# A post-norm attention and expert layer on one core: expert units loaded four ahead, a seventh half batch in expert order, side work between attention tiles in parts

## The chip, the cores and the metric

The program runs on 1 core of one Trainium2 chip. The metric is the device time of one execution in microseconds (us), and lower is better. The engines are TensorE (PE, with its weight loads shown as PEld), VectorE (DVE), ScalarE (ACT), GpSimd (POOL) and SyncE (SP), whose queue issues most DMAs.

## The reference

x has 4 batches of 1024 rows of 128 numbers, all in float32. One layer of attention and one of experts, each with a residual sum and a layer norm behind it:

```python
q, k, v = x @ Wq, x @ Wk, x @ Wv
latent = (k + v) @ W_down_kv
k_rec, v_rec = latent @ W_up_k, latent @ W_up_v
# 16 heads of 8 numbers
scores = clip(einsum(qh, kh) * scale) * exp(-0.0001 * |i - j|)
x = layernorm(x + (softmax(scores) @ vh) @ Wo)
top_logits, top_idx = top_k(x @ w_router, 2)          # 8 experts
h1 = x_e @ fc1_w[e]; proj, gate = split(h1)
out_e = (silu(proj) * gate) @ fc2_w[e]                # for the two experts of a row
moe = sum over the two of softmax(top_logits) * out_e
shared = (silu(x @ gate_w) * (x @ up_w)) @ down_w
x = layernorm(x + moe + shared)
```

## The kernel before, in words

The rows are cut into 8 **half batches** of 512 rows, c = 0 to 7. The kernel has two stages.

**Attention.** The work is 256 **tiles**, 32 in each half batch (32c + t, t = 0 to 31). A tile is one group of four heads (a quad, of which a half batch has four) and 128 keys against 512 queries. TensorE makes the scores into PSUM (L819), VectorE multiplies the diagonal band of a **crossing** tile (L1293; the tiles whose keys lie in the half batch of the queries), ScalarE makes two exponentials of 128x1024 (L714), and TensorE adds the probabilities times V into one output bank (L832). TensorE runs one tile ahead with its scores; three pairs of PSUM banks hold them. Keys and queries come in a split form with the decay multiplied in: GpSimd makes it (`split`, L535 to L537, twelve operations of a half batch), SP stores it into `stack_dram` (L386) and loads it back a quad at a time (`load_quad`, L379 and L381), two quads ahead of their use. SP issues in program order, and so the load of a quad stands behind the stores that the loop puts ahead of it (step g == 1 of each half batch).

**Side work.** Between tiles TensorE does one piece of other work for the half batch before (d = c - 1) and the one two ahead (p = c + 2), all in one PSUM bank, each piece after VectorE has taken the one before (`side`, `side_kept`). `beside` (from L897) places them by tile: `xT` (turn x, t = 1), the output turns `o` (t = 2, 10, 18, 26), `q` and `k` (projections of 512 columns, t = 3 and 5), `a` (turn, 4), `wo` (output projection, 6), `v` (7), `x` (turn the normed rows, 12), `lg` (router, 14), `norm` (15) and `cnt` (17). `cnt` counts the rows of each expert and waits for `chosen_ready`, which VectorE sets after it has found the two experts of each row (`route_lanes` and `choose`, taken at t = 16). GpSimd norms the rows (`ln1_rows`, L555 to L558) and makes a power (L568).

**Expert order.** For half batches 0 to 5 the rows are sorted by expert. The first GROUP is half batches 0 to 3 in 40 blocks of 128 rows, the second 4 and 5 in 24 blocks. When the counts are known VectorE works out each row's place (`order_counts` to `order_experts`), and GpSimd scatters rows into `sorted_dram` by indirect DMA (`send`, L574, 48 of 128 rows each). Half batches 6 and 7 are dense: every expert is applied to all rows and weighted.

**The ring stage.** After the last tile TensorE walks through a list `work` of pieces; each result takes the next of the eight PSUM banks in turn and is counted by `ring_ready`. The pieces: a **unit** is four blocks of the sorted rows (turn of its rows L774, up L980, down L994), a **shared** piece is the shared expert of one half batch (L985 with 8 matmul instructions, down L998 and L999), a **dense** piece one expert on 512 rows (L985 with 4, down L996). In the trace each float32 matmul stands as two. There are 16 units, 16 dense and 8 shared pieces. ScalarE copies and makes the silu (L738, L743, L748), VectorE multiplies (`hidden`, L1396) and adds dense and shared results (L1404, L1410). Five short steps of half batch 7 (`LAST_STEPS`) stand among the first pieces; `x` there waits for GpSimd's `ln1_rows(7)`.

A unit needs its rows (`load_rows`, L459, 256 KB) and its blocks' weights (`load_weights`, L466, four DMAs of 192 KB, each addressed by a register). There are two buffers of each, u % 2. SP's loop, in order, for unit u: load the rows of u + 2 (after the turn of u), load the weights of u + 2 (after the down of u), load 3 registers (L452), wait for ScalarE's copy of unit u's result, store it (L481). After ten units are stored GpSimd gathers the results of half batch 0 (`fetch`, L586, 8 indirect DMAs a half batch, each held back until the ring has come to an entry), then 1, 2, 3, and after all units 4 and 5; two half batches of gathered rows fit. VectorE weighs and adds them (`combine`, L1444) and makes statistics, GpSimd a power (L563, L564), ScalarE scales the rows (L724), SP stores them (L485).

## Time and profile before

| what | us |
|---|---|
| time, median of 3 runs | 804.7 |
| lowest and highest of the 3 | 801.01, 807.33 |
| the profiled execution, its own time | 802.82 |
| span of the profiled execution, first to last instruction | 800.9 |
| busy in it: PE, ACT, DVE, POOL | 675.2, 545.7, 333.2, 264.7 |

The time around the span is 802.82 - 800.9 = 1.9 us. In the trace the first exponential starts at 54.4 us and the last tile's matmuls end at 601.9 us, so the attention stage takes 547.5 us and the ring stage with the end 199.0 us. A row of the timeline gives start, duration, engine and line, the operation with its operands, how many instructions are merged, and in brackets how long the engine was idle before and which instruction or DMA released it. A row of the chain of waits has start, duration and what the chain went through there; its durations are exclusive, so that they can be summed. Line numbers are those of the kernel before.

### The profile page before, as it was taken

Reading aid. Unit: us, or ns where it says so; the run is one execution under the profiler, and the core shown is the slowest. Engines: PE = TensorE matmul, PEld = TensorE weight load, DVE = VectorE, ACT = ScalarE, POOL = GpSimd, SP = SyncE. Lnnn points to the kernel's source line nnn. Section 1 sums busy time; section 2 is a strip of 40 time slices with the busy share of each in tenths; the row PEclk is TensorE's granted clock in tenths of the full one; section 3 lists DMA queues with packets and bytes.
Section 4 is the critical chain, followed back from the end, with each engine's and each line's share of the span. In section 5 each row is a group of like instructions: output and inputs, shape, how many; then the busy total and the mean of one; then the engine's idle time right before and its main releaser. Section 6 shows DMA issues by size and latency. Waiting matters only on the chain.

```text
span 800.9 us, 12944 instructions
## 1 busy us (share of the span) xinstructions
PE 675.2 (84%) x4821; PEld 305.5 (38%) x4821; DVE 333.2 (42%) x989; ACT 545.7 (68%) x636; POOL 264.7 (33%) x250
## 2 busy tenths in 40 slices
PE   5029997999999999999999999999999878758980
PEld 3013322333333233333323333423337667646540
DVE  2913422443542244354525344433434412134883
ACT  2027996879789887978988899899993322223342
POOL 2800531720360171046227543044000100245672
PEclk9559998999999999999999999999999999888996
DMA  3799282274255227425423955243203665564131
GB/s 110 244 335 393 95 279 103 95 295 163 93 192 190 80 99 298 157 92 201 184 89 118 330 194 168 79 163 141 80 11 109 186 187 154 171 188 138 44 85 50
DMA packets 72883, 127.83 MB, mean 160 GB/s; under 512 B 6064, under 2 KB 48368, under 8 KB 72816
## 3 DMA queue, kind: packets, MB, share of 16 engines
q1 hardware_dynamic: 69216, 120.47, 43.4%
q0 software_dynamic: 3072, 6.30, 2.8%
q8 instruction: 40, 0.66, 0.3%
q10 hardware_dynamic: 528, 0.18, 0.1%
q14 instruction: 27, 0.22, 0.1%
HBM read 79.74 MB, written 48.76 MB: 160 GB/s over the span
## 4 chain that ended last, share of the span: by engine, by line
PE 59%; DVE 8%; issue 5%; ACT 4%; SPq 3%; DMA 3%; POOL 1%; another core or an unknown queue 0%; ACTq 0%; DVEq 0%
PE ps L832 22%; PE ps L819 16%; PE ps L985 5%; PE ps L774 4%; ACT probs L714 4%; PE ps L980 3%; DVE ps L1293 2%; DMA keys<-sorted_dram 2%; SPq L466 2%; PE ps L996 1%; PE ps L853 1%; PE ps L874 1%; DVE osb L1297 1%; PE ps L879 1%; PE ps L998 1%
## 5 line engine op out<-in xcount | busy, mean ns | idle before, releaser
L714 ACT ACTIVATE probs<-ps 128x1024 f32<-128x1024 f32 x512 | 479.3, 1053 | 103.8 <-DVE ps L1293 79.9
L832 PE MATMUL ps<-probs,V 128*9 128x512 f32 x2048 | 273.2, 606 | 1.2 <-ACT probs L714 0.4
L819 PE MATMUL ps<-queries,keys 32*128 32x512 f32 (+3 forms) x1408 | 199.5, 417 | 52.1 <-DMA queries<-stack_dram 39.2
L819 PEld LDWEIGHTS ps<-queries,keys 32*128 32x128 f32 x1408 | 98.4, 186 | 241.0 <-ACT probs L714 146.9
L1293 DVE TENSOR_TENSOR ps<-ps,cpk 128x256 f32<-128x256 f32 x256 | 103.2, 429 | 183.0 <-PE ps L819 177.1
L535 POOL TENSOR_TENSOR stage<-qk,rows_sb 128x512 fp32r<-128x512 f32 x28 | 36.8, 1314 | 183.9 <-DVE qk L1154 168.7
L586 POOL DMA_INDIRECT queries<-result_dram,slots x48 | 48.7, 1016 | 90.2 <-PE ps L980 68.1
L743 ACT ACTIVATE probs<-ps 128x512 f32<-128x512 f32 x48 | 28.5, 596 | 68.0 <-PE ps L985 33.4
L574 POOL DMA_INDIRECT sorted_dram<-xn,slots x48 | 47.0, 979 | 74.2 <-ACT probs L714 60.6
L1396 DVE TENSOR_TENSOR probs<-probs,ps 128x512 f32<-128x512 f32 x48 | 32.8, 687 | 86.0 <-PE ps L980 57.0
L985 PE MATMUL ps<-xnT,stage 128*128 128x512 f32 x128 | 59.0, 593 | 0.0
L1297 DVE COPY osb<-ps 128x512 f32<-128x512 f32 x32 | 22.1, 691 | 85.7 <-PE ps L832 85.7
L832 PEld LDWEIGHTS ps<-probs,V 128*9 128x9 f32 x2048 | 30.5, 88 | 58.5 <-issue 39.2
L980 PE MATMUL ps<-probs,keys 128*128 128x128 f32 x256 | 39.2, 319 | 0.0
L537 POOL TENSOR_TENSOR stage<-pool_f,stage 128x512 fp32r<-128x512 f32 x28 | 37.1, 1323 | 2.2
L980 PEld LDWEIGHTS ps<-probs,keys 128*128 128x128 f32 x256 | 37.6, 233 | 0.0
L536 POOL TENSOR_TENSOR pool_f<-qk,rows_sb 128x512 f32<-128x512 f32 x28 | 37.1, 1326 | 0.0
L555 POOL TENSOR_TENSOR small<-small 128x4 f32<-128x4 f32 x8 | 8.2, 1020 | 80.3 <-DVE small L1173 80.3
L545 POOL TENSOR_TENSOR squares<-qk 128x512 bf16<-128x512 f32 x16 | 17.0, 1082 | 51.1 <-DVE nmax L1269 50.9
L774 PE MATMUL ps<-cpk,keys 128*128 128x128 f32 x64 | 11.2, 303 | 26.7 <-DMA keys<-sorted_dram 26.7
L985 PEld LDWEIGHTS ps<-xnT,stage 128*128 128x128 f32 x128 | 22.5, 191 | 20.0 <-issue 18.6
L738 ACT ACTIVATE probs<-ps 128x512 f32<-128x512 f32 x16 | 9.5, 595 | 27.5 <-PE ps L774 27.5
(155 smaller groups left out, 540.4 us busy)
## 6 DMA issues: line engine op xcount, KB each, us to landing
stack_dram<-stage SPq DMA_DIRECT2D x64, 512.0 KB, 6.5
keys<-stack_dram SPq DMA_DIRECT2D x32, 1024.0 KB
queries<-stack_dram SPq DMA_DIRECT2D x32, 512.0 KB
keys<-expert_dram SPq DMA_DIRECT2D x64, 192.0 KB
sorted_dram<-y_pre SPq DMA_DIRECT2D x1, 4096.0 KB, 18.5
keys<-sorted_dram SPq DMA_DIRECT2D x16, 256.0 KB, 3.2
result_dram<-probs SPq DMA_DIRECT2D x16, 256.0 KB
x_tok<-in_L_attn_x SPq DMA_DIRECT2D x8, 256.0 KB, 5.8
```

What stands on the lines that cost most here:

```text
L535: rest(nc.gpsimd.tensor_tensor(hi, src, tab, ALU.mult))
L536: link(nc.gpsimd.tensor_tensor(pool_f[:, v, :], src, tab, ALU.mult))
L537: rest(nc.gpsimd.tensor_tensor(lo, pool_f[:, v, :], hi.bitcast(F32), ALU.subtract))
L574: pool.indirect_dma_start(out=sorted_dram, out_offset=bass.IndirectOffsetOnAxis(ap=slots[:, s, k:k + 1], axis=0), in_=xn[:, k // CT, tok(k ...
L586: pool.indirect_dma_start(out=gathered[:, c % 2, s, tok(t)], out_offset=None, in_=result_dram[0:rows, :], in_offset=bass.IndirectOffsetOnA ...
L714: nc.scalar.activation(probs[:, m % 3, 2 * j:2 * j + 2, :], ps[:, 2 * s:2 * s + 2, :], ACT.Exp, scale=SCALE).then_inc(exp_done, 1)
L774: last = nc.tensor.transpose(dst[:, tok(t)], src[:, tok(t)], ident)
L819: last = mm(bank[2 * s + i][:, lo:hi], keys[rows, u, kt // CT, v, tok(kt % CT)], queries[rows, u, v, lo:hi], start=True, stop=True)
L832: last = mm(bank[OUT_BANK][32 * i:32 * i + HD + 1, :], V[:, c // 2 % 2, kt, 4 * (Q % QUADS) + i, :], probs[:, m % 3, i, :], start=(kt == 0 ...
L980: last = mm(dst[:, tok(b)], wblk[:, u % 2, b, k * F:(k + 1) * F], xT_blk[:, u % 2, tok(b)], start=True, stop=True)
L985: last = mm(dst, up_sb[:, e, k * F:(k + 1) * F], xnT[:, c, :], start=True, stop=True)
L1293: tt(d, d, diag_fix.unsqueeze(1).to_broadcast([P, 2, P]), ALU.mult).then_inc(diag_done, 1)
```

## The change

- The second group is half batches 4, 5 and 6 in 32 blocks, 72 blocks in all. So there are 18 units, 8 dense and 8 shared pieces; half batch 6 has a `cnt` in attention (in half batch 7) and 8 more `send`s and gathers.
- Rows and weights of units have four buffers (`AHEAD`), in `pool_f`, `rows_sb`, parts of `keys` and `V`. The first two rows and the first weights are loaded before the last tile. 32 registers are loaded in half batch 7, and 4 a unit in the loop for ten units (3 before, for eleven).
- The pieces stand in another order, with all units ahead of all dense pieces, and so do the steps of half batch 7, the places of the combines and the gathers' hold-backs.
- The 24 sends of the second group stand in the ring stage, held back by `ring_ready`, and ahead of `ln1_rows(7)` on GpSimd. The 32 of the first group stand in half batches 5 and 6.
- Side work is placed by a table, `side_places`: `q`, `k`, `v`, `wo` and `lg` are done in two halves in neighbouring tiles, most jobs stand in tiles that don't cross, and `cnt` comes three tiles after `choose`. GpSimd splits the queries of p in one go before the keys; the splits of the keys stand behind `ln1_rows`.

```diff
-GROUPS = [(0, 4, 0, 40), (4, 6, 40, 64)]
+GROUPS = [(0, 4, 0, 40), (4, 7, 40, 72)]
...
+        AHEAD = 4
+        wblk = [w.rearrange("p (k n) -> p k n", k=UB) for w in (
+            rows_sb[:, :, :].rearrange("p v s -> p (v s)")[:, 0:UB * 3 * F], kflat[:, 0:UB * 3 * F], kflat[:, UB * 3 * F:2 * UB * 3 * F],
+            V[:, :, :, :, :].rearrange("p b t h d -> p (b t h d)")[:, 0:UB * 3 * F])]
...
+        def side_places(c):
...
+            z = 0 if c % 2 else 4
+            places = {("xT", p): (0 if c % 2 else 2,), ("o", 4 * d + 3): (z + (1 if c % 2 else 0),),
+                      ("q", p): (z + 2, z + 3) if c % 2 else (z + 1, z + 2), ("a", d): (6 if c % 2 else 7,),
+                      ("k", p): (z + 8, z + 9), ("wo", d): (z + 10, z + 11), ("o", 4 * c): (z + 13,),
+                      ("x", d): (z + 16,), ("norm", p): (z + 17,), ("lg", d): (z + 18, z + 19), ("o", 4 * c + 1): (z + 21,),
+                      ("cnt", d): (z + 24,), ("v", p): (z + 25, z + 26), ("o", 4 * c + 2): (z + 27,)}
...
-        for u in range(2 * GROUP - 2, UNITS, 2):
-            work += [("dense", GROUP, u // 2 - GROUP + 1), ("unit", u), ("unit", u + 1)]
...
+        shared_before = {0: 0, 4: 1, 8: 2, 12: 3, 15: 4}
+        work = []
+        for u in range(UNITS):
+            if u in shared_before:
+                work += [("shared", shared_before[u])]
+            work += [("unit", u)]
+        work += [("shared", c) for c in range(len(shared_before), GROUP)]
+        for c in range(GROUP, NCH):
+            work += [("dense", c, e) for e in range(E)] + [("shared", c)]
...
-        LAST_STEPS = {0: "o", 1: "a", 2: "wo", 4: "x", 5: "lg"}
+        LAST_STEPS = {0: "o", 1: "a", 2: "wo", 7: "x", 9: "lg"}
+        COMBINE_AFTER = {17: [0], 20: [1], 23: [2], 25: [3], 30: [4], len(work): [5, 6]}
...
-            n = ring["dn", "unit", GROUPS[0][3] // UB - 1][0] + (2 * CT * c + i) * 8 // 5
+            n = ring["dn", "unit", (FIRST_UNITS if c < GROUPS[0][1] else UNITS) - 1][0] + (2 * CT * (c % GROUPS[0][1]) + i) * 3 // 2
...
+            load_rows(0)
+            load_rows(1)
+            sp.wait_ge(experts_joined, 32)
+            load_weights(0)
+            sp.wait_ge(scores_ready, 2 * TILES)
+            load_weights(1)
+            load_rows(2)
+            load_weights(2)
+            load_rows(3)
+            sp.wait_ge(pv_done, TILES)
+            load_weights(3)
...
-                if u + 2 < UNITS:
-                    load_rows(u + 2)
-                    load_weights(u + 2)
-                if u < 11:
-                    load_registers(3)
+                if u + AHEAD < UNITS:
+                    load_rows(u + AHEAD)
+                    load_weights(u + AHEAD)
+                if u < 10:
+                    load_registers(4)
...
+            pool.wait_ge(slots_ready, 3)
+            for k in range(GROUPS[0][1] * CT, GROUP * CT):
+                send(k, ring_ready, 3 * (k - GROUPS[0][1] * CT))
             ln1_rows(LAST)
             gap_power(LAST)
...
+            def project(p, n, part):
+                dst = side(("qk"[n], p)) if part == 0 else bank[SIDE_BANK]
+                cols = slice(part * HALF // 2, (part + 1) * HALF // 2)
+                last = mm(dst[:, cols], wfold[:, 2, :] if n else Wq_sb[:, :], xT[:, p % 2, cols], start=True, stop=True)
```

On TensorE in half batch 1, from the router matmul (`Wr_sb`) to the count (`chosen`), the order before; a pair of L819 and L832 rows is a tile:

```order
160 L879 MATMUL ps<-Wr_sb,xnT 128x8 x4
161 L819 MATMUL ps<-queries,keys 128x512 x4
162 L832 MATMUL ps<-probs,V 9x512 x4
163 L865 MATMUL ps<-squares,head_sum_h 32x512 x2
164 L819 MATMUL ps<-queries,keys 128x512 x4
165 L832 MATMUL ps<-probs,V 9x512 x4
166 L819 MATMUL ps<-queries,keys 128x512 x4
167 L832 MATMUL ps<-probs,V 9x512 x4
168 L886 MATMUL ps<-chosen,cpk 128x40
```

The same place after, up to the count; L809 and L822 are now the tile's lines, and L764 is an output turn:

```order
184 L822 MATMUL ps<-probs,V 9x512 x4
185 L764 MATMUL ps<-cpk,osb 128x128 x4
186 L809 MATMUL ps<-queries,keys 128x384 x2
187 L809 MATMUL ps<-queries,keys 128x128 x2
188 L809 MATMUL ps<-queries,keys 128x384 x2
189 L809 MATMUL ps<-queries,keys 128x128 x2
190 L822 MATMUL ps<-probs,V 9x512 x4
191 L809 MATMUL ps<-queries,keys 128x512 x4
192 L822 MATMUL ps<-probs,V 9x512 x4
193 L809 MATMUL ps<-queries,keys 128x512 x4
194 L822 MATMUL ps<-probs,V 9x512 x4
195 L880 MATMUL ps<-chosen,cpk 128x40
```

The router matmul is now two halves (rows 174 and 177 of the same list), and five tiles lie between the second half and the count where three lay before.

On SP in the loop of the ring stage, the end of one unit's weights up to the next rows, before (`block_e` is what a register is loaded from):

```order
189 L466 ISA
190 L466 DMA keys<-expert_dram 128x384
191 L452 TENSOR_LOAD block_e
192 L452 ISA x2
193 L452 TENSOR_LOAD block_e
194 L452 ISA x2
195 L452 TENSOR_LOAD block_e
196 L452 ISA x2
197 L481 DMA result_dram<-probs 128x4x128
198 L459 DMA keys<-sorted_dram 128x4x128
```

The same place after:

```order
206 L423 ISA
207 L423 DMA rows_sb<-expert_dram 128x384
208 L409 TENSOR_LOAD block_e
209 L409 ISA x2
210 L409 TENSOR_LOAD block_e
211 L409 ISA x2
212 L409 TENSOR_LOAD block_e
213 L409 ISA x2
214 L409 TENSOR_LOAD block_e
215 L409 ISA x2
216 L479 DMA result_dram<-probs 128x4x128
217 L416 DMA pool_f<-sorted_dram 128x4x128
```

One register load more stands in each turn of the loop, and what is loaded is four units ahead.

On GpSimd from the last sends to the first gathers, before:

```order
126 L574 DMA sorted_dram<-xn,slots 8192x128 x16
127 L555 TENSOR_TENSOR small<-small 128x4
128 L557 TENSOR_TENSOR xn<-y_pre,small 128x512
129 L558 TENSOR_TENSOR xn<-xn,small 128x512
130 L568 TENSOR_TENSOR small<-small 128x4
131 L555 TENSOR_TENSOR small<-small 128x4
132 L557 TENSOR_TENSOR xn<-y_pre,small 128x512
133 L558 TENSOR_TENSOR xn<-xn,small 128x512
134 L568 TENSOR_TENSOR small<-small 128x4
135 L586 DMA queries<-result_dram,slots 128x128 x16
```

And after:

```order
129 L566 TENSOR_TENSOR small<-small 128x4
130 L573 DMA sorted_dram<-xn,slots 9216x128 x24
131 L553 TENSOR_TENSOR small<-small 128x4
132 L555 TENSOR_TENSOR xn<-y_pre,small 128x512
133 L556 TENSOR_TENSOR xn<-xn,small 128x512
134 L566 TENSOR_TENSOR small<-small 128x4
135 L585 DMA queries<-result_dram,slots 128x128 x16
```

The last sends, 24 of them, now stand directly ahead of the norm of half batch 7's rows.

## Rows read from the trace of the kernel before

**Rows 1.** Busy time by stretch; columns: length, PE, PEld, DVE, ACT, POOL, clock, DMA share, GB/s.

```profile
54.40:124.60 70.20, 61.79 (x450) 20.70 (x454) 22.65 (x51) 59.65 (x65) 19.11 (x16) 0.91 0.76 273
...
335.40:404.30 68.90, 64.55 (x504) 23.60 (x500) 32.27 (x101) 60.16 (x66) 29.15 (x26) 1.00 0.45 164
404.30:474.00 69.70, 65.60 (x504) 23.51 (x500) 28.85 (x87) 60.06 (x66) 36.84 (x35) 0.98 0.48 170
...
538.10:600.90 62.80, 61.15 (x476) 20.81 (x468) 23.73 (x79) 59.72 (x65) 12.00 (x13) 1.00 0.25 91
601.90:734.00 132.10, 105.43 (x665) 88.90 (x662) 40.54 (x107) 38.13 (x64) 25.18 (x26) 0.90 0.55 163
734.00:783.00 49.00, 43.90 (x201) 26.96 (x199) 41.46 (x151) 17.58 (x37) 34.66 (x38) 1.00 0.27 73
```

**Rows 2.** The chain of waits in two neighbouring tiles without side work.

```profile
520.45 0.98 PE ps L832 x8
522.28 0.98 PE ps L832 x8
```

**Rows 3.** Timeline of PE at the end of half batch 0.

```profile
123.67 0.80 PE L819 MATMUL ps<-queries,keys 32*128 32x512 f32 x4 [4.99 <-DMA queries<-stack_dram]
```

**Rows 4.** Timeline of SP there: the load of the quad behind the stores.

```profile
99.66 12.14 SPq L386 DMA_DIRECT2D stack_dram<-stage  x8
111.92 1.14 SPq L379 DMA_DIRECT2D keys<-stack_dram  x1
```

**Rows 5.** Timeline of PE at the count of half batch 5.

```profile
446.07 0.41 PE L886 MATMUL ps<-chosen,cpk 128*128 128x40 f32 x2 [1.47 <-issue]
...
448.99 1.12 PE L774 MATMUL ps<-cpk,osb 128*128 128x128 f32 x4
```

**Rows 6.** Waits of the ring stage: total us, times, longest.

```profile
PE ps L774 <- DMA keys<-sorted_dram: 26.7, 7, 6.6
```

**Rows 7.** The chain of waits in the ring stage: TensorE's pieces.

```profile
610.12 0.22 PE ps L999 x2
...
627.67 1.79 PE ps L980 x16
...
633.93 0.89 PE ps L994 x8
634.82 0.44 PE ps L774 x4
635.26 3.44 PE ps L985 x8
...
642.99 3.38 PE ps L980 x16
...
739.75 1.72 PE ps L985 x4
```

**Rows 8.** Timeline of SP: weights, result and rows in one turn of the loop.

```profile
635.01 1.93 SPq L466 DMA_DIRECT2D keys<-expert_dram  x4
638.66 0.39 SPq L481 DMA_DIRECT2D result_dram<-probs  x1
639.09 0.50 SPq L459 DMA_DIRECT2D keys<-sorted_dram  x1
```

**Rows 9.** The chain of waits: two register loads of SP.

```profile
653.58 0.26 SPq L452
654.13 0.26 SPq L452
```

**Rows 10.** Timeline of POOL: the first of the three operations that norm half batch 7.

```profile
619.36 1.01 POOL L555 TENSOR_TENSOR small<-small 128x4 f32<-128x4 f32 x1 [47.54 <-DVE small L1173]
```

**Rows 11.** The chain of waits at the end: last gathers, last combine.

```profile
779.89 1.00 POOL queries L586
...
781.19 3.85 DMA queries<-result_dram,slots
785.07 1.15 DVE qk L1444 x4
```

More of the change, by code:

```diff
@@ L618, in _ @@
                     split(0, p, 0)
+                    split(0, p, 1)
+                    split_end()
+                    pool.wait_ge(side_kept, numbers["k", p])
+                    squares_of(p)
                 if d >= 0:
@@ L1462, in _ @@
                     last_step(k)
-                if k and work[k - 1] == ("shared", GROUP):
-                    dve.wait_ge(ring_by_dve, ring["dn", "shared", GROUP][2])
-                    ln2_statistics(GROUP)
-                if k in COMBINE_AFTER:
-                    combine(COMBINE_AFTER[k])
-                    ln2_statistics(COMBINE_AFTER[k])
+                for c in COMBINE_AFTER.get(k, []):
+                    combine(c)
+                    ln2_statistics(c)
             dve.wait_ge(ring_by_dve, ring["dn", "shared", LAST][2])
```

384 lines of the change are left out of this document (169 added, 215 removed).

## The prediction

> **What bounds the kernel now.** I read the busy time by stretch first [rows 1]. The attention stage (54.4 to 601.9 us) is TensorE and ScalarE together: in half batch 7 (538.1 to 600.9) PE is busy 61.2 and ACT 59.7 of 62.8 us. The chain of waits has neighbouring plain tiles 522.28 - 520.45 = 1.83 us apart, with TensorE in it [rows 2]. 32 such tiles make 58.6 us. Half batch 7 takes 4.2 us more than that, half batch 5 (404.3 to 474.0) takes 69.7 - 58.6 = 11.1 more, half batch 4 10.3. That excess is side work and what it makes late. Two places in it are plain waits. At the end of half batch 0 TensorE stands 4.99 us for a quad [rows 3], whose load SP issued at 111.92, behind eight stores that took from 99.66 to 111.8 [rows 4]. And at the count of half batch 5 it stands 1.47 us; the output turn after it takes 1.12 us [rows 5].
>
> The ring stage (601.9 to 800.9) is 199.0 us. To 734 PE is busy 105.4 of 132.1 us at a granted clock of 0.90 [rows 1]. Its waits are seven for the rows of a unit, 26.7 us together, the longest 6.6 [rows 6]. The timeline of SP says why: the rows of the unit after next are issued only behind the weights, the register loads and the result of the unit before (639.09 behind 638.66 behind 635.01) [rows 8], and TensorE has by then done what it had. After such a wait the up of a unit takes 3.38 us where 1.79 is usual: the lower clock level, 1.2 GHz in place of 2.4 [rows 7]. From 734 to 783 VectorE is busy 41.5 of 49 us [rows 1], and the end is gathers, combine, statistics and scaling: the last gather lands at 785.07, 15.8 us before the end of the span [rows 11].
>
> **The change part by part: attention.**
> (a) The quad wait. The keys of half batch 2 are split later now (their projection stands at tiles 12 and 13), but the queries' stores go out before and only four stores stand ahead of the load. At about 2 us a tile the key split is over near 97 us, its four stores at 12.14 / 8 = 1.5 us each near 103, and the load is needed at about 118. The 4.99 us go, and about 0.9 us of slow tiles behind them: -5.9.
> (b) The count waits. By the order the count now stands five tiles behind the router's matmuls instead of three, and three behind `choose`. Odd half batches lose 1.47 us and the lower clock behind it. The clock of 0.98 over 69.7 us [rows 1] is 2.8 us at half speed, 1.4 us lost. 2.9 in each of half batches 1, 3 and 5, 8.6; in the even ones, where the excess is 0.8 smaller, I take 0.5 each for three (bounds 0 and 1). -10.
> (c) Side work in halves. No row shows a halved job. It may cost 0.2 us more for the second weight load and start at each of five jobs (1 us in each of six half batches, +6); it may save, since the smaller bites fit in the slack of three score buffers: the eight jobs of half batch 7 stand apart already, and of the eight, five turns at 4 x 0.15, two of 1 us and the router, about 5.6 us of matmuls cost 4.2, a quarter hidden. A quarter of 11 in six is -16. I take 0, between the ends: part of that quarter is in the measured excess already. Both ends stay for the range, +6 and -10.
> (d) One more count in half batch 7: +1.2. The later split in even half batches ends about 11 us before its quad is issued late; nothing waits by my sum.
> Sum -15 (bounds -6, if halves only cost and part of the clock loss stays, and -25): the last tile ends at 587.
>
> **The ring stage.** TensorE's pieces [rows 7]: unit 0.44 + 1.79 + 0.89 = 3.12; dense 1.72 + 0.89 = 2.61 (its down has as many instructions as a unit's); shared 3.44 + 8 x 0.22 = 5.2; the five last steps 3.1. Before: 16 x 3.12 + 16 x 2.61 + 8 x 5.2 + 3.1 = 136.4. After: 18 x 3.12 + 8 x 2.61 + 41.6 + 3.1 = 121.7. So 14.7 us of work go.
> The waits for rows go too: the rows of u + 4 are issued three units ahead of their turn. What is late next?
> - SP. A turn of its loop costs 4 x 0.52 (weights; 1.93 with the gap to the next) + 4 x 0.55 (two register loads are 654.13 - 653.58 apart [rows 9]) + 0.43 + 0.55 = 5.3 us; TensorE needs a unit each 3.12 + 5.2 / 4 = 4.4. Four units in hand at the start last for about 4 / (1 - 4.4 / 5.3) turns, over 20, and the register loads end after ten. It holds, with some small waits about units 8 to 13. But SP stores the results, and so unit 9 is stored late: first turn at 587 + 11.9 (turn, shared, two ups, down, steps) + 4.7 = 603.7, nine turns of 5.3 on: 651.5, landed near 654.5 (3 us, an estimate by the gather's 3.85 with its issue [rows 11]).
> - DMA. A unit moves 256 + 768 + 256 KB = 1.31 MB. The stretch to 734 moved 163 GB/s at a share of 0.55, so 296 at 1.0 [rows 1]. That is 4.4 us a unit, just TensorE's pace, with 0.22 us for each of 24 sends and 32 gathers beside. Over 18 units about 92 us against 88 for TensorE: a few us.
> - GpSimd's row norm. The last send waits for ring entry 35, and `x` of half batch 7 is entry 38, 0.9 + 0.9 us of matmuls later. Behind the send (1.3) come three operations of 1.1 [rows 10]: x is late by 1.3 + 3.3 - 1.8 = 2.8 to 3.7 us. It was hidden before.
> - The first combine. It stands in VectorE's queue behind piece 17, which TensorE reaches near 587 + 80 = 667. Eight gathers from 654.5 at 1.30 (781.19 - 779.89) are issued by 665, the last lands 2.9 later, combine and statistics are 4: VectorE is back at 672 at best, and all `hidden` products wait behind it. TensorE stands 5 us, up to 13 if gathers queue behind loads. I take 8.
> TensorE's end: 587 + 121.7 + 3.5 + 8 + 3.4 (slow clock after both) + 4 (SP, DMA) + 3 (VectorE, 85% busy in the dense pieces) = 730.6.
> - GpSimd's chain is longer. From 654.5: 56 x 1.30 = 72.8, six powers between at 1.5 = 9, so the last is issued at 736.3 and has landed at 739.2. Then the 15.8 us of the end [rows 11], since the fifth half batch is combined by then: 755.0.
> Span 755; with 1.9 us around it **757 us**, against 802.8 of the profiled execution, 46 less: 15 in attention and 31 in the ring stage. To the median of the runs shown, 804.7, the profiled one stands 2 lower; I leave that inside the range.
>
> **A rule against it.** In the stretch to 783 gathers stand at 1.00 us and 1.30 apart beside a VectorE that is 85% busy [rows 1, 11]. The Trainium skill, SBUF — State Buffer, section SBUF: two separate sides, says that a VectorE instruction in a two-port mode keeps GpSimd from writing the descriptors of its DMAs. By that rule the gathers would crawl beside combines; by the rows they don't, and the sum stays. What it would do here is the third rival.
>
> **The rivals.**
> 1. *Attention gains only its plain waits.* Halves cost their 6 us and the count's clock loss stays: 587 becomes 596 and the time 766. For it: TensorE is 95% busy there and a job's time is a job's time. Against: half batch 7 hides a quarter. 0.17.
> 2. *The unit stage becomes a queue.* SP's turns and the DMA engines, at 0.9 and more, stretch each other (a turn of 5.3 becomes 6.3, as the weights' issue is slower when the queue is full: the stores at 1.5 us each show that [rows 4]). Unit 9 is stored 9 us later, the combine wait doubles, and GpSimd's chain begins at 664: 757 + 9 to 757 + 20, say 771. For it: demand equals what is shown. Against: loads are four ahead. 0.17.
> 3. *The gathers pace the end, slower than before.* One mechanism: GpSimd's 56 gathers in one chain. The sum is 654.5 + 56 g + 9 + 2.9 + 15.8 + 1.9, and passes 802.8 at g = 2.1 us. In the kernel before 48 gathers took the 88 us from 694 to 782, 1.8 each, but held back by the ring. If descriptors wait for VectorE or the queue for 1 us each, g = 2.3 and the time is 813. Against: 1.30 apart where nothing holds them back. 0.05.
>
> **How the numbers follow.** Forecast 0.61, rivals 0.17, 0.17 and 0.05. The forecast's own range is 743 to 772 (attention -10 or +9, ring -5 or +8). The range for all is 742 to 782: the upper end takes in most of rival 2. A measurement of this kernel tells about 1% from no change. Faster by over 1%: all but rival 3 and a share for what I haven't seen: 0.93; within 1%: 0.03; slower: 0.04.
>
> **What would show it.** Right: no quad wait at the end of half batch 0; no clock below 0.99 in half batches 1 to 5; last tile near 587; no wait of 2 us or more for a unit's rows; a wait of about 3 us at the turn of half batch 7's normed rows; TensorE idle 5 to 13 us about the down of unit 14, with VectorE behind the first combine; gathers 1.3 us apart from about 655 to 736 and the span ending 16 us behind the last landing. Wrong: an attention stage of 540 us or more; SP's turns above 6 us; waits for weights (up of a unit behind `expert_dram`); quads late in even half batches, where the key split now ends later; or the end set by TensorE.

## The result and the profile after

The changed kernel took 782.2 us (median of 4 runs, 779.2 to 784.6), the kernel before beside it 806.0 (801.0 to 813.6): ratio 0.972, 95% interval 0.965 to 0.979. It is faster by 24 us, where 46 were forecast; 757 was the number, and 782 the upper end of the range, which the 782.2 pass by 0.2. The profiled execution has a span of 778.4 us, against the 755 of the sum.

| | before | forecast | after |
|---|---|---|---|
| last tile of attention ends | 601.9 | 587 | 597.9 |
| unit 9's results stored | 690.1 | 651.5 | 671.65 |
| gathers, first to last issue | 693.8 to 781.2 | 654.5 to 736.3 | 675.0 to 758.6 |
| span | 800.9 | 755 | 778.4 |

Of the 23.4 us that are missing, 10.9 are attention's; the ring stage (598 to 778.4) took 180.5 where 168 were forecast, 12.5 more. The busy time by stretch, for half batches 0, 4, 5, 6, 7 and the first part of the ring stage, answers to [rows 1]:

```profile
54.40:123.60 69.20, 63.98 (x450) 20.69 (x454) 21.31 (x49) 60.05 (x65) 19.02 (x16) 0.89 0.79 275
325.80:394.90 69.10, 66.51 (x504) 23.98 (x500) 25.65 (x81) 60.68 (x66) 21.14 (x18) 0.95 0.45 157
394.90:462.70 67.80, 64.17 (x512) 23.73 (x508) 33.42 (x108) 60.33 (x65) 32.06 (x29) 1.00 0.46 169
462.70:533.30 70.60, 65.04 (x484) 22.77 (x480) 23.48 (x87) 60.22 (x66) 24.65 (x26) 0.95 0.41 142
533.30:596.80 63.50, 61.65 (x490) 22.09 (x482) 27.57 (x97) 59.84 (x65) 5.27 (x5) 1.00 0.29 102
597.90:734.00 136.10, 113.39 (x745) 93.52 (x742) 53.09 (x161) 46.86 (x85) 70.04 (x72) 0.92 0.66 196
```

Half batch 5 is 1.9 us shorter, half batch 4 as long as it was (0.95 of the clock: 1.2 GHz from 366.8 to 373.7), and half batch 6 is 6.5 us longer than the 64.1 of before. The timeline of PE names what came in place of the waits that went:

```profile
90.89 0.61 PE L859 MATMUL ps<-squares,head_sum_h 128*32 128x512 bf16 x2 [3.21 <-POOL squares L543]
...
122.95 0.51 PE L809 MATMUL ps<-queries,keys 32*128 32x512 f32 x4 [0.19 <-DMA queries<-stack_dram]
...
230.63 0.50 PE L809 MATMUL ps<-queries,keys 32*128 32x384 f32 x4 [1.31 <-ACT probs L704]
...
262.01 0.66 PE L764 MATMUL ps<-cpk,x_tok 128*128 128x128 f32 x4 [1.37 <-DVE a_tok L1157]
...
318.52 0.66 PE L764 MATMUL ps<-cpk,osb 128*128 128x128 f32 x4 [1.07 <-DVE vstat L1119]
```

The quad wait of 4.99 us [rows 3] is down to 0.19 (122.95). But at tile 15 of half batch 0 `norm 1`, now directly behind `norm 0`, waits 3.21 us for squares that GpSimd starts only when `norm 0` is kept. In odd half batches the turn of x stands directly behind the third output turn (262.01), and that one directly behind the values (318.52): one side bank, so TensorE waits until VectorE has emptied it. In even ones VectorE's statistics stand ahead of a diagonal tile's scaling (230.63). In half batch 6 VectorE sits idle 4.41 us by the timeline, though the matmuls that made the first of its scores began at 467.12 and those for the second ended at 468.10. A releaser called `remote` is one that the profile doesn't name:

```profile
467.12 0.98 PE L809 MATMUL ps<-queries,keys 32*128 32x384 f32 x8
...
471.33 0.76 DVE L1288 TENSOR_TENSOR ps<-ps,cpk 128x256 f32<-128x256 f32 x2 [4.41 <-remote]
```

In the ring stage up to 700 PE's timeline has three waits of over 1 us, none of them for rows (26.7 us before [rows 6]):

```profile
616.07 3.63 PE L975 MATMUL ps<-probs,V 128*128 128x128 f32 x16 [2.11 <-ACT probs L728]
...
639.01 1.09 PE L764 MATMUL ps<-cpk,xn 128*128 128x128 f32 x4 [5.34 <-POOL xn L556]
...
694.51 2.05 PE L989 MATMUL ps<-keys,probs 128*128 128x128 f32 x8 [8.84 <-ACT probs L738]
```

The third is at the down of unit 14, behind the first combine. VectorE's timeline has the combine, the last step of its statistics and the product that the down needs:

```profile
687.67 2.31 DVE L1439 SCALAR_TENSOR_TENSOR x_tok<-queries,small,x_tok 128x128 f32<-128x128 f32 x8 [8.38 <-issue]
...
691.55 0.32 DVE L1168 TENSOR_SCALAR small<-small 128x4 f32<-128x4 f32 x1
693.67 0.69 DVE L1391 TENSOR_TENSOR probs<-probs,ps 128x512 f32<-128x512 f32 x1 [1.81 <-remote]
```

SP's timeline shows the stores of units 0, 1, 4, 5 and 9; GpSimd's gathers follow as one line of the view by source:

```profile
615.89 0.40 SPq L479 DMA_DIRECT2D result_dram<-probs  x1
...
621.87 0.39 SPq L479 DMA_DIRECT2D result_dram<-probs  x1
...
639.71 0.39 SPq L479 DMA_DIRECT2D result_dram<-probs  x1
...
649.58 0.39 SPq L479 DMA_DIRECT2D result_dram<-probs  x1
...
671.65 0.39 SPq L479 DMA_DIRECT2D result_dram<-probs  x1
```

```profile
L585 POOL DMA_INDIRECT queries<-result_dram,slots x56: 992/997/1133, 675.0 to 758.6; - x56
```

Unit 5 follows unit 4 by 9.9 us, since the wait for x stands between them; then come turns of 5.4 us (one of 5.9).

### The profile page after: what moved, and what is told of

Same layout as the page of the kernel before. It is cut to its first block, busy times and chain, and to the rows that moved or that the text cites. A ratio compares the mean times of both kernels' runs of the same rounds, so it can differ in the third digit from the quotient of the medians.

```text
span 778.4 us, 12970 instructions
## 1 busy us (share of the span) xinstructions
PE 658.6 (85%) x4815; PEld 296.5 (38%) x4815; DVE 316.5 (41%) x958; ACT 546.6 (70%) x634; POOL 281.0 (36%) x266
## 4 chain that ended last, share of the span: by engine, by line
PE 69%; DVE 11%; ACT 7%; DMA 4%; issue 3%; POOL 2%; another core or an unknown queue 1%; SPq 0%; ACTq 0%; DVEq 0%; POOLq 0%
PE ps L822 26%; PE ps L809 18%; ACT probs L704 7%; PE ps L980 5%; PE ps L764 5%; PE ps L975 4%; DVE ps L1288 3%; PE ps L989 2%; PE ps L844 2%; DMA queries<-stack_dram 2%; PE ps L868 1%; DVE small L1161 1%; DVE osb L1292 1%; PE ps L991 1%
## 5 line engine op out<-in xcount | busy, mean ns | idle before, releaser
L822 PE MATMUL ps<-probs,V 128*9 128x512 f32 x2048 | 274.4, 609 | 0.8 <-ACT probs L704 0.5
L809 PE MATMUL ps<-queries,keys 32*128 32x512 f32 (+3 forms) x1408 | 194.5, 418 | 48.4 <-DMA queries<-stack_dram 31.9
L809 PEld LDWEIGHTS ps<-queries,keys 32*128 32x128 f32 x1408 | 95.0, 187 | 209.0 <-ACT probs L704 133.1
L573 POOL DMA_INDIRECT sorted_dram<-xn,slots x56 | 54.9, 980 | 73.2 <-ACT probs L704 35.5
L585 POOL DMA_INDIRECT queries<-result_dram,slots x56 | 57.3, 1023 | 45.4 <-PE ps L994 25.1
L733 ACT ACTIVATE probs<-ps 128x512 f32<-128x512 f32 x42 | 24.8, 599 | 40.4 <-PE ps L980 26.1
L822 PEld LDWEIGHTS ps<-probs,V 128*9 128x9 f32 x2048 | 30.5, 88 | 57.6 <-issue 43.2
L1391 DVE TENSOR_TENSOR probs<-probs,ps 128x512 f32<-128x512 f32 x42 | 28.4, 685 | 56.6 <-PE ps L975 16.3
L980 PE MATMUL ps<-xnT,stage 128*128 128x512 f32 x96 | 44.0, 593 | 0.0
L738 ACT ACTIVATE probs<-ps 128x512 f32<-128x512 f32 x18 | 10.8, 597 | 37.7 <-PE ps L989 10.6
L553 POOL TENSOR_TENSOR small<-small 128x4 f32<-128x4 f32 x8 | 8.2, 1022 | 59.4 <-DVE small L1168 59.4
L566 POOL TENSOR_TENSOR small<-small 128x4 f32<-128x4 f32 x8 | 8.1, 1008 | 58.8 <-DVE small L1188 54.9
L728 ACT ACTIVATE probs<-ps 128x512 f32<-128x512 f32 x18 | 10.7, 595 | 23.0 <-PE ps L764 15.7
L764 PEld LDWEIGHTS ps<-cpk,osb 128*128 128x128 f32 x128 | 13.9, 144 | 32.4 <-issue 15.9
L764 PE MATMUL ps<-cpk,osb 128*128 128x128 f32 x128 | 21.6, 292 | 3.3 <-DVE vstat L1119 3.2
```

Source lines behind the costliest of these rows:

```text
L573: pool.indirect_dma_start(out=sorted_dram, out_offset=bass.IndirectOffsetOnAxis(ap=slots[:, s, k:k + 1], axis=0), in_=xn[:, k // CT, tok(k ...
L585: pool.indirect_dma_start(out=gathered[:, c % 2, s, tok(t)], out_offset=None, in_=result_dram[0:rows, :], in_offset=bass.IndirectOffsetOnA ...
L764: last = nc.tensor.transpose(dst[:, tok(t)], src[:, tok(t)], ident)
L809: last = mm(bank[2 * s + i][:, lo:hi], keys[rows, u, kt // CT, v, tok(kt % CT)], queries[rows, u, v, lo:hi], start=True, stop=True)
L822: last = mm(bank[OUT_BANK][32 * i:32 * i + HD + 1, :], V[:, c // 2 % 2, kt, 4 * (Q % QUADS) + i, :], probs[:, m % 3, i, :], start=(kt == 0 ...
L980: last = mm(dst, up_sb[:, e, k * F:(k + 1) * F], xnT[:, c, :], start=True, stop=True)
```

## The experiments

Eighteen runs, in six sets, each set on one chip (A to F) beside the kernel before. Four columns of the table are read from the timelines: attention from the first score matmul to the end of the last tile, unit 9's store behind that end, the gathers from first to last issue, and the span behind the last gather's issue.

| run | chip | attention | store | gathers | end | median |
|---|---|---|---|---|---|---|
| before | - | 548.9 | 88.1 | 87.4 | 19.8 | 803 to 809 |
| changed | - | 544.9 | 73.7 | 83.6 | 19.8 | 782.2 |
| e1 old places | A | 551.7 | 72.2 | 83.4 | 19.8 | 790.1 |
| e2 norms apart | A | 535.9 | 73.6 | 83.2 | 19.7 | 772.3 |
| e3 row norm early | A | 542.4 | 71.7 | 83.4 | 19.8 | 775.2 |
| e4 registers early | A | 539.9 | 73.9 | 83.5 | 19.8 | 778.3 |
| e5 both of these | B | 537.1 | 64.4 | 81.1 | 19.8 | 763.1 |
| e6 all four | B | 524.3 | 63.9 | 81.4 | 19.7 | 748.6 |
| e7 two buffers | B | 539.3 | 111.3 | 102.3 | 19.8 | 830.8 |
| e8 combines later | C | 542.2 | 73.6 | 86.9 | 19.8 | 780.5 |
| e9 old order | C | 540.0 | 78.3 | 76.1 | 20.0 | 780.1 |
| e10 all four, later | C | 526.4 | 70.9 | 87.2 | 19.8 | 767.2 |
| e11 = e6 | D | 526.8 | 71.1 | 84.0 | 19.8 | 762.3 |
| e12 = e10 | D | 527.1 | 68.8 | 88.9 | 19.9 | 767.2 |
| e13 = changed | E | 542.0 | 73.1 | 83.3 | 19.8 | 777.8 |
| e14 = e5 | E | 542.2 | 70.6 | 83.0 | 19.8 | 774.8 |
| e15 = e6 | E | 524.8 | 71.5 | 83.1 | 19.7 | 761.0 |
| e16 shared before unit 3 | E | 526.2 | 68.0 | 83.4 | 19.8 | 758.5 |
| e17 four result buffers | F | 527.3 | 71.1 | 83.7 | 21.5 | 763.4 |
| e18 and late registers | F | 527.0 | 64.1 | 85.2 | 20.0 | 759.5 |

Runs of two chips can be compared only roughly: the changed kernel took 782.2 and 777.8 us, and e6, e11 and e15, one kernel on three chips, lie 13.6 us apart. Only chip E had the changed kernel beside others, so e1 to e4 are read by the columns of their profiled executions, not by their times alone.

**e1, the old places.**

```diff
-            places = {("xT", p): (0 if c % 2 else 2,), ... ("cnt", d): (z + 24,), ... ("o", 4 * c + 2): (z + 27,)}
+            places = {("xT", p): (1,), ("o", 4 * d + 3): (2,), ("q", p): (3,), ("a", d): (4,), ("k", p): (5,), ("wo", d): (6,),
+                      ("v", p): (7,), ("o", 4 * c): (10,), ("x", d): (12,), ("lg", d): (14,), ("norm", p): (15 if c else 19,),
+                      ("cnt", d): (17,), ("o", 4 * c + 1): (18,), ("o", 4 * c + 2): (26,)}
```

> The changed kernel with its side jobs whole and at the tiles of the kernel before (transfer of rows by GpSimd in the order of before too); groups, four-ahead and the order of the pieces stay. Theory A (the places gave only the 4.0 us that attention's end moved): attention lasts 547.5 us again (from 54.4 on) instead of 543.5, the 4.99 us wait for the quad after half batch 0 and the 3.4 us of half clock at every count are back, the ring stage stays at 180.5, the time is 786 us. Theory B (the places gave most of the 24 us, the ring stage little): 795 us or more.

Attention took 551.7 us, the time is 790.1. The seven waits of the count are back, as its list of waits says, one of the odd ones in PE's timeline:

```profile
PE ps L877 <- DVE chosen L1206: 8.3, 7, 1.6
```

```profile
165.33 0.39 PE L877 MATMUL ps<-chosen,cpk 128*128 128x40 f32 x2 [1.56 <-DVE chosen L1206]
```

The quad wait came back at 1.80 us only. Nine executions of kernels with the new places and without the edits of e2 and e6 have an attention of 537.1 to 544.9, mean 541.1; the two with the old ones 548.9 and 551.7. So the places are worth about 9 us, and the profiled execution of the changed kernel, which showed 4, was the longest of the nine. The theory that the ring stage gave most stands: e1, which has the ring's part alone, is 14.0 us under the kernel before on its chip (804.1; 95% interval of the difference 9 to 22). The 786 were 4 too low.

**e2, the norms apart.**

```diff
-                places.update({("norm", 0): (14,), ("norm", 1): (15,)})
+                places.update({("norm", 0): (10,), ("norm", 1): (15,)})
```

> Norm 0 at tile 10 of half batch 0 instead of 14, so five tiles ahead of norm 1. Theory A (norm 1 waited for GpSimd's squares, which start when norm 0 is kept): TensorE's idle 3.21 us at tile 15 and the half clock of 90.4 to 97.2 are gone, half batch 0 takes 63.6 us instead of 69.2, the time is 776.6 us. Theory B (another wait of half batch 0 takes its place, such as the third norm or the quad): half batch 0 stays above 67 us and the time at 780 to 782.

Theory A. Half batch 0 is 63.3 us long (69.2 before the edit), by the busy time of its stretch, and the clock stays at 2.4 GHz from 61.4 to 361.7. In the nine executions with this edit half batch 0 takes 63.3 to 64.6 us, in the nine with the two norms next to each other 68.6 to 69.7, 5.4 us apart in the mean:

```profile
54.50:117.80 63.30, 61.21 (x448) 20.52 (x446) 21.30 (x49) 59.66 (x64) 19.09 (x16) 0.95 0.85 297
```

**e3 and e4, the row norm and the register loads.**

```diff
             for k in range(GROUPS[0][1] * CT, GROUP * CT):
+                if k == GROUPS[0][1] * CT + 8:
+                    ln1_rows(LAST)
                 send(k, ring_ready, 3 * (k - GROUPS[0][1] * CT))
-            ln1_rows(LAST)
```

> GpSimd's row norm of half batch 7 stands ahead of its last 8 sends (after 16 of 24). Theory A (the 5.34 us wait at x of half batch 7 delays every later store of results and with them the gathers): the wait and its half clock are gone, unit 9's store and the first gather are 4.5 to 8 us earlier (gathers from 667 to 670.5 us), the time is 775 to 778 us. Theory B (SP's turns of 6.2 us pace the stores whatever TensorE does): unit 9's store stays within 1 us of 671.65 and the time at 781 to 783.

```diff
-                    load_registers(8)
+                    load_registers(10)
...
                     load_rows(u + AHEAD)
+                    if u == 0:
+                        load_registers(12)
                     load_weights(u + AHEAD)
-                if u < 10:
-                    load_registers(4)
...
+                if 3 < u < 9:
+                    load_registers(4)
```

> SP reads 40 block numbers in half batch 7 (was 32), 12 while it waits for the first unit, and the rest behind the stores of units 4 to 8: none ahead of a store. Theory A (SP's turns of 6.2 us, 4 reads of 0.55 us in each, hold the stores back): the first store comes at 613.7 instead of 615.9, the turns fall to 4.5 to 5.5 us outside the x wait, unit 9's store comes 4 to 6 us earlier, the time is 776 to 778 us. Theory B (TensorE's pieces with the x wait pace the stores): unit 9's store moves by under 2 us, the time is 780 to 782.

Each alone did little for the store: 71.7 and 73.9 us behind attention's end, where the changed kernel has 73.7 and 73.1. In e3 the wait for x is gone, and the nine turns from the first store to unit 9's still take 53.9 us, against 55.8. In e4 unit 4 is stored 37.1 us behind attention's end, where e3 needs 43.4, but then the wait for x takes it back (5.9 us in PE's timeline), and unit 5 comes 12.6 us later:

```profile
633.35 1.09 PE L766 MATMUL ps<-cpk,xn 128*128 128x128 f32 x4 [5.91 <-POOL xn L558]
```

```profile
629.58 0.45 SPq L479 DMA_DIRECT2D result_dram<-probs  x1
...
642.20 0.42 SPq L479 DMA_DIRECT2D result_dram<-probs  x1
```

Counted from the start of the span both would be theory A's or close to it: unit 9's store at 666.80 in e3 and 666.35 in e4, against 671.65, and 775.2 and 778.3 us. But attention, whose side jobs neither edit moves, ended 2.8 and 5.5 us earlier in them; without that the store moves by 2.1 us in e3 and not at all in e4. So the store speaks for theory B in e4, and nearly so in e3. That each was held by the other's pace is argued here and tried in e5.

**e5, both together, and e14, the same again beside the changed kernel (e13).**

> The two changes of the earlier row norm and of the earlier block numbers together. Alone they moved unit 9's store, counted from attention's end, from 74.8 to 73.4 us and to 74.9 us. Theory A (two paces stand beside each other, SP's turns of 5.4 us or more and TensorE's wait for x, and either alone keeps the store where it is): together the store comes 60 to 66 us after attention's end, the first gather 3.5 us behind it, the time is 765 to 770 us. Theory B (a third thing paces it, the 768 KB of weights of each unit or the copies by ScalarE): the store stays 70 us or more behind attention's end, the time is 773 to 776 us.

> The changed kernel unchanged, beside the next three on one chip. One kernel (all four changes) took 748.6 us on one chip and 762.3 us on another, with before at 806 on both. Theory A (the changed kernel has slack where that differs, since SP's turns and the x wait pace it): 780 to 785 us, unit 9's store 74 to 76 us behind attention's end. Theory B (the changed kernel differs by chip as well): outside 775 to 790 us.

> The earlier row norm and the earlier block numbers together, which took 763.1 us against 782.2, compared now on one chip. Theory A (the gain of the two together is of the program): 765 to 769 us or less, unit 9's store 65 to 67 us behind attention's end. Theory B (half of it was the chip: at the start of the ring VectorE and ScalarE stand still 4 to 5 us with their inputs ready, as in the last three runs): 772 to 777 us, the store 70 to 73 us behind attention's end.

The changed kernel again (e13) took 777.8 us, its store 73.1 behind attention's end: under theory A's 780, inside theory B's bounds. e5 was 763.1 us, its store 64.4 behind attention's end, as theory A has it. On chip E the same kernel took 774.8 beside 777.8, store 70.6 against 73.1: theory B of e14. So the two edits together are worth 3.0 us there, by medians of four executions each that overlap at one (778.99 of e14), and it is open what they are worth on chip B, where the changed kernel didn't run. What is left in the way is tried in e17 and e18.

**e6, all four.** The edits of e2, e3 and e4, and neighbours set apart:

```diff
-                      ("cnt", d): (z + 24,), ("v", p): (z + 25, z + 26), ("o", 4 * c + 2): (z + 27,)}
+                      ("cnt", d): (z + 24,), ("v", p): (z + 25, z + 26), ("o", 4 * c + 2): (29 if c % 2 else 26,)}
+            if c % 2:
+                places.update({("o", 4 * d + 3): (4,)})
+            if c and c % 2 == 0:
+                places.update({("wo", d): (12, 13), ("k", p): (14, 15)})
```

> Both of these, norm 0 at tile 10 of half batch 0, and neighbours set apart: in odd half batches o(4d+3) at tile 4 and o(4c+2) at 29, in even ones o(4c+2) at 26, and the output projection ahead of the key projection so that VectorE's row statistics no longer precede a diagonal tile. Theory A (each wait between neighbours costs what the trace shows, 1.4 and 1.5 us in odd half batches, 1.3 in even ones): odd half batches 65.0 to 66.0 us instead of 67.8, even ones 1 to 2 us shorter, half batch 0 at 63.6; the time is 5.6 + 8 us below the run before, 752 to 757 us. Theory B (a job costs its time wherever it stands): half batches 1 to 5 unchanged, the time is 759 to 764 us.

748.6 us, ratio to before 0.927 (0.923 to 0.932), 14.5 us under e5 on the same chip; on chip E the pair e14 and e15 stands 13.8 apart. So this part holds on either chip. Half batches 1, 2 and 3 (67.6, 66.6 and 68.0 in the changed kernel) are:

```profile
120.00:186.00 66.00, 63.79 (x508) 23.39 (x504) 28.35 (x88) 60.30 (x65) 21.21 (x18) 1.00 0.47 170
186.00:251.10 65.10, 63.67 (x508) 23.79 (x504) 25.65 (x80) 60.51 (x65) 21.18 (x18) 1.00 0.48 169
251.10:317.20 66.10, 63.88 (x508) 23.39 (x504) 28.79 (x91) 60.38 (x65) 21.18 (x18) 1.00 0.47 170
```

Theory A: a job costs by its neighbours, 1.5 to 2 us in each of these half batches. (The 748.6 are 3.4 under its range, as e5 beside it is 2 under its own.)

**e7, two buffers, and e9, the old order with four.**

```diff
-        AHEAD = 4
+        AHEAD = 2
```

> The changed kernel with two buffers of rows and weights instead of four. Theory A (the ring stage's 18.5 us came mostly from four-ahead, since SP's chain of rows, weights and result then has slack): units take 5 to 6 us each for lack of rows, unit 9's store comes 8 us or more later, the time is 790 to 800 us. Theory B (the groups and the order of pieces gave it, with GpSimd's gathers as the bound): within 3 us of 782.

830.8 us, 25 above the kernel before and far above either theory. The new order puts unit behind unit, with few other pieces between; with two buffers TensorE waits for rows and weights at nearly each, by the list of waits from 590 to 740:

```profile
PE ps L759 <- DMA pool_f<-sorted_dram: 30.4, 7, 8.1
PE ps L970 <- DMA keys<-expert_dram: 15.7, 3, 5.5
...
PE ps L970 <- DMA rows_sb<-expert_dram: 5.5, 1, 5.5
```

e9 is the counterpart: half batch 6 dense again, 16 units, and the pieces in the order of before, with four buffers and the new places.

```diff
-GROUPS = [(0, 4, 0, 40), (4, 7, 40, 72)]
+GROUPS = [(0, 4, 0, 40), (4, 6, 40, 64)]
...
-        for u in range(UNITS):
-            if u in shared_before:
-                work += [("shared", shared_before[u])]
-            work += [("unit", u)]
+        work = [("shared", 0), ("shared", 1), ("unit", 0), ("unit", 1)]
...
+        for u in range(2 * GROUP - 2, UNITS, 2):
+            work += [("dense", GROUP, u // 2 - GROUP + 1), ("unit", u), ("unit", u + 1)]
```

> The changed kernel (its places for the side jobs, its four buffers) with the groups and the order of pieces of before: half batch 6 dense, 64 blocks, 16 units. Theory A (four-ahead is what gains, by the 26.7 us of waits for rows in the ring of before; the new order only costs, since it brings unit after unit and runs into SP's turns and 8 more gathers): 766 to 776 us, faster than the changed kernel. Theory B (half batch 6 by expert and the new order gain the 8 us that their pieces are shorter): 786 to 792 us.

780.1 us beside 780.5 of e8 (the changed kernel with later combines) on chip C: neither theory's number. The waits for rows are gone here too; the store is 4.7 us later than e8's, and the 48 gathers are 10.8 us shorter in all than e8's 56. So four buffers are the gain, and the groups and the order are worth nothing that shows beside them, though by the forecast's sum they take 14.7 us of work from TensorE. A few us either way stay open: the kernel beside e9 is e8 and not the changed one (later combines cost 5 us in e12), and e9's four executions lie between 773.7 and 784.0.

**e8, the combines later.**

```diff
-        COMBINE_AFTER = {17: [0], 20: [1], 23: [2], 25: [3], 30: [4], len(work): [5, 6]}
+        COMBINE_AFTER = {19: [0], 22: [1], 25: [2], 27: [3], 31: [4], len(work): [5, 6]}
```

> The changed kernel with its first five combines two, two, two, two and one piece later. Theory A (the chain of GpSimd's gathers sets the end, TensorE's 8.84 us wait at the first combine only moves its idle time): the wait falls to 3 us or less, the first gather and the last stay where they are relative to attention's end (78.2 and 161.8 us), the time stays within 2 us of 782. Theory B (the wait is on the path): the last gather and the end come 5 to 9 us earlier, 773 to 777 us.

The time is theory A's, but the edit did not do what it was for: TensorE's wait is still 8.14 us, now ahead of the combine (VectorE's product that it waits for starts at 688.66, the combine at 693.29), and GpSimd, VectorE, TensorE and ScalarE go on at 689.39, 688.66, 689.50 and 690.15, all within 1.5 us. So this run does not tell what the combine's wait is worth, and what held four engines is open. VectorE's other input, ScalarE's silu, was done at 682.84, 5.8 us before the product. The changed kernel's trace has the same event: there the statistics end at 691.87, and VectorE, ScalarE, GpSimd and TensorE go on at 693.67, 693.78, 694.40 and 694.51. The gathers took 3.3 us longer than the changed kernel's, since, by the program, those of half batch 2 wait for the first combine's buffer.

```profile
688.66 0.69 DVE L1391 TENSOR_TENSOR probs<-probs,ps 128x512 f32<-128x512 f32 x1 [13.67 <-remote]
...
693.29 0.87 DVE L1439 SCALAR_TENSOR_TENSOR x_tok<-queries,small,x_tok 128x128 f32<-128x128 f32 x3
```

**e10, e11 and e12.**

> The run with all four changes (748.6 us), and the combines later as well. Theory A (gathers set the end): TensorE's 10.0 us at the first combine shrinks to 4 us or less, the gathers keep their 81.4 us from first to last, the time is 747 to 750 us. Theory B (TensorE's wait is on the path): 740 to 744 us. Rival C (the later combine holds back the gathers of half batch 2, which need its buffer): 751 to 755 us.

> The kernel of the run that took 748.6 us, once more, beside the next one on one chip. Of the 18.5 us between that run and the one with later combines, 7.3 arose between attention's end and unit 9's store, where both have the same instructions, and 5.8 between the first and the last gather. Theory A (the 7.3 us are of that chip or of those executions): this run and the next have unit 9's store at the same distance from attention's end, within 2 us, and lie 3 to 8 us apart. Theory B (they are of the program): this run is at 747 to 751 us again, its store 64 to 65 us behind attention's end.

> The run with later combines once more. Theory A: 3 to 8 us above the run beside it, all of it between the first and the last gather (85 to 88 us instead of 81.4). Theory B: 16 to 20 us above it again, with unit 9's store 71 to 72 us behind attention's end.

e10 took 767.2, 18.5 more than e6, so more than any theory. e11 and e12, the two kernels on one chip, took 762.3 and 767.2: theory A. Later combines cost 5 us, all in the gathers (88.9 against 84.0 us; the store comes 2.3 us earlier). The other 13.6 us are not the program's: e6 and e11 are the same kernel. Their profiled executions differ by 9.6 us, of which 7.2 lie between attention's end and unit 9's store, and the timelines of the two at unit 4's result and x of half batch 7 show how: in e11 ScalarE and VectorE stand still for 4 to 5 us with their inputs ready,

```profile
615.91 0.60 ACT L747 ACTIVATE probs<-ps 128x512 f32<-128x512 f32 x1 [5.18 <-remote]
...
617.37 0.69 DVE L1430 COPY xnT<-ps 128x512 f32<-128x512 f32 x1 [4.33 <-PE ps L998]
```

in e6 both start as soon as the matmuls that they read are done (608.57 and 609.00):

```profile
608.60 0.60 ACT L747 ACTIVATE probs<-ps 128x512 f32<-128x512 f32 x1 [1.19 <-PE ps L998]
...
609.04 0.69 DVE L1430 COPY xnT<-ps 128x512 f32<-128x512 f32 x1 [0.64 <-PE ps L773]
```

**e15 and e16.**

```diff
-        shared_before = {0: 0, 4: 1, 8: 2, 12: 3, 15: 4}
+        shared_before = {0: 0, 3: 1, 8: 2, 12: 3, 15: 4}
```

> All four changes on this chip. Theory A: 747 to 751 us as in the first run. Theory B (the standstills at the start of the ring are here too): 758 to 766 us.

> All four changes, and the shared pieces of half batch 1 ahead of unit 3 instead of unit 4, so that TensorE has 5.2 us of other work before it needs unit 3. Theory A (TensorE's 2 to 7 us before the up of unit 3 are a wait for its rows and weights, which start last): the wait is gone, 2 to 5 us faster than the run beside it. Theory B (engines stand still there whatever the order): the wait shows at another piece, within 2 us of the run beside it.

e15: 761.0, theory B. e16: 758.5, 2.5 us less. TensorE's wait at the up of unit 3 (1.94 us in e15) is gone, and one of 4.53 stands at unit 7's instead, behind ScalarE's copy; the time is theory A's, the mechanism B's.

```profile
619.72 3.75 PE L984 MATMUL ps<-probs,V 128*128 128x128 f32 x16 [4.53 <-ACT probs L737]
```

**e17 and e18, what paces the stores.**

```diff
-        y_blk = pflat[:, 2 * HALF:4 * HALF].rearrange("p (u s) -> p u s", u=2)
+        y_buf = [y_blk[:, 0, :], y_blk[:, 1, :], ... rows_sb ... [:, UB * 3 * F:UB * 3 * F + HALF],
+                 ... V ... [:, UB * 3 * F:UB * 3 * F + HALF]]
...
-                    if u >= 2:
-                        act.wait_ge(results_stored[u % 2], 16 * (u // 2))
+                    if u >= 4:
+                        act.wait_ge(results_stored[u % 4], 16 * (u // 4))
```

> All four changes, and four buffers for a unit's results instead of two. In two traces ScalarE's copy of a unit's result starts 0.1 us behind the landing of the store two units before in 10 of 16 units (the store takes 4 to 6 us to land beside the loads, 2.5 alone), and everything ScalarE has to do behind it waits along. Theory A (this is the third pace, and the standstills of the other chips are the same wait with its record missing): no such waits are left, unit 9's store comes 62 us or less behind attention's end on any chip, the time is 740 to 748 us. Theory B (SP's turns pace the stores and the copies only wait in their shade): the store stays at 64 to 72 us, the time at 748 to 762 us.

```diff
-                if 3 < u < 9:
+                if 7 < u < 13:
                     load_registers(4)
```

> The same, with the last 20 block numbers read behind the stores of units 8 to 12 instead of 4 to 8, so that no read stands ahead of unit 9's store but 4 of them. Theory A: no more than 2 us under the run beside it. Theory B (SP's turns of 5.8 us in units 5 to 9, 2.2 of them reads, are the pace): turns of 4 to 5 us there, the store 5 to 8 us earlier than in the run beside it, the time 4 to 8 us below it.

e17 is theory B: ScalarE's copies no longer wait for a landing, and the store stays 71.1 us behind attention's end, the time is 763.4, 1.4 over its range. So the wait for a result buffer stood in the shade of something else. In e18 the median is 3.9 us lower, just short of theory B's lower bound of 4, with executions of the two that overlap (755.6 to 762.9, and 762.1 to 765.4). In the profiled executions the store is 7.0 us earlier, but 3.8 of them arose before unit 4, where both have the same instructions; the other 3.2 are the edit's: from unit 4 to 9 the stores are 5.3 us apart in the mean, against 5.9 in e17; theory B had them at 4 to 5. The reads in SP's turns are worth 3 to 4 us, and that is all of the pace that I could name.

## Why the forecast was half right

- *(a), the quad wait: right.* 4.99 us became 0.19.
- *(b), the counts: right.* No wait stands at a count any more, half batch 5's clock is 1.00, and e1 brings 8.3 us of such waits back. (Half batch 4, where the sum had no loss of clock, fell to 0.95.)
- *(c), "side work in halves: I take 0": the step that failed in attention.* I asked what half a job costs and not what stands next to a moved one. The sum's terms give 64.3 us for half batch 0, 339.7 for 1 to 5, 63.7 for 6 and 63.9 for 7; measured were 69.2, 339.1, 70.6 and 63.6. The 4.9 us over in half batch 0 are the two norms, shown by e2. In half batches 1 to 5 the other pairings (output turns directly behind x or the values, statistics ahead of a diagonal tile) cost 1.5 to 2 us each, shown by e6, but there the sum came out all the same: the price of the neighbours was made up by gains that it had not counted, so that part was right by luck. The 6.9 over in half batch 6 are the larger half of the error, and their cause is open: 64.5 us on chip B, 67.5 to 70.6 in the other executions of these instructions, with VectorE's stand of 4.41 in the longest. With the edits of e2 and e6 attention falls from 541 to 526 us in the mean, 23 under the kernel before where I had said 15. Rival 1's 596 was nearest to the 597.9, for another reason.
- *The durations: right.* SP's later turns are 5.4 us against 5.3, and the first store came 18.0 us behind attention's end, against 16.7.
- *"Nine turns of 5.3 on: 651.5": the step that failed in the ring stage.* They took 55.8 us instead of 47.8. I had forecast the late x (3 us; it was 5.34, and the lower clock behind it) and charged it to TensorE's end alone. But SP's turns are the chain that sets the start of the gathers, and a turn across TensorE's wait took 9.9 us, 4.6 over; the first three, at 6.0 to 6.4, are 2.5 over. Rival 2 has this size (turns of 6.3; measured 6.2 in the mean, the store 9.2 later than the sum has it), but its mechanism doesn't show: the issue of a unit's weights took 1.97 to 2.54 us within these turns, against 1.93. Taking the two delays away gives back only part. Without the wait for x the nine turns take 53.9 us (e3); with both mended 49.8 and 50.2 on chip B and 52.1 to 55.8 elsewhere; only e18, with the last reads later still, has 47.5. Compared on one chip it is 3.0 us (e14 against e13) and 3.9 (e18 against e17). What holds the rest of the turns is open.
- *"GpSimd's chain is longer": right.* 83.6 us from first to last gather against 81.8, and 19.8 behind it against 18.7. In all eighteen runs 19.7 to 21.5 us follow the last gather's issue, seventeen of them between 19.7 and 20.0, while 18.8 (e9) to 29.1 (e8) follow TensorE's end: the gathers set the end.
- *The first combine: right in size, in part by luck.* TensorE stood 8.84 us against 8, with VectorE's combine at 687.67 ahead of the product that it waits for. But 1.8 of these us lie behind the statistics, where VectorE, ScalarE and GpSimd stand too, and e8 has a wait of 8.14 at the same piece with the combine behind it. In e6 (10.01 us) the product does follow the statistics at once. That the wait costs nothing at the end is not shown (e8).
- *The third rival: not so.* The gathers' median is 997 ns beside a busy VectorE. The rule of the Trainium skill, SBUF — State Buffer, section SBUF: two separate sides, that VectorE can hold up GpSimd's descriptors, shows in no run here; whether the combine's operations are of the two-port kind that it speaks of, no run tells.

The ring stage's 12.5 us over are 1.3 (first store) + 8.0 (turns) + 0.3 (landing) + 1.8 (gathers) + 1.1 (end); with attention's 10.9 that is the whole 23.4 of the profiled execution. 3 to 4 us of the 10.9 are of this one execution, the longest of nine.

## What to carry to other kernels

When a table moves jobs, look at each pair that become neighbours, and at the buffer or engine that both need, before pricing the jobs themselves. A late operand delays every engine behind the one that waits: carry it through to the chain that sets the end. Two limits of about the same pace can hide each other, so take both away before calling either free; and compare runs on one chip.

## What the hardware showed

- *One kernel, two times.* All four edits took 748.6 us on chip B, 762.3 on D and 761.0 on E, each within 3.5 to 5.8 us from lowest to highest, while the kernel before took 805.7, 806.2 and 808.9 there. The difference lies at the start of the ring stage: unit 9's store 63.9 us behind attention's end, or 71.1 and 71.5. In e11's timeline ScalarE and VectorE stand for 4 to 5 us there with their inputs done, and in e6's they don't; in e8 four engines go on together after such a stand. In e15 no such stand is named, and TensorE's matmuls come in pieces with "issue" before them. The three traces of chip B (e5, e6, e7) differ from all others in one more thing: the landing of each of the 18 stores is recorded and no wait has a releaser without a name, while the others record no store's landing in full and have such waits. Whether the two belong together, and why the stands come, is open: no run tried it.
- *Half batch 6* took 64.5 to 70.6 us in executions of the same instructions, 64.5 twice on chip B and 67.5 or more elsewhere, with the 4.41 us stand of VectorE in one of them.
- *A store of results* (256 KB) landed 3.6 to 6.6 us after its issue beside the loads, and 2.3 to 2.7 when they were over (e5, e6).
